# Delta-rule attention without the first segment's reading of an empty memory, with the memory's start multiplied in bf16

## The reference, cut to what matters

```python
def step(carry, seg):
    mem, z = carry
    qq, kk, vv = seg
    sigma_q = elu(qq) + 1.0
    att_dot = softmax(causal(qq @ kk.T / scale)) @ vv
    att_mem = sigma_q @ mem / (sigma_q @ z)
    sigma_k = elu(kk) + 1.0
    delta = vv - sigma_k @ mem / (sigma_k @ z)
    mem_new = mem + sigma_k.T @ delta
    z_new = z + sigma_k.sum(axis=-2)
    att = beta * att_mem + (1.0 - beta) * att_dot
    return (mem_new, z_new), att @ Wo
mem0 = zeros((H, DK, DV)); z0 = ones((H, DK, 1)) / DK
```

## Time and profile before

| what | us |
| --- | --- |
| median of 3 runs | 709.62 |
| lowest and highest of them | 709.52, 710.14 |
| the profiled execution | 709.2 |
| its span, first to last instruction | 706.7 |

### The profile page before, as it was taken

The page is one execution under the profiler, slowest core; times in us unless marked ns, Lnnn a source line. Parts: engine busy times, 40 slices in busy tenths (PEclk is TensorE's granted clock), DMA queues, the critical chain, the costliest instruction groups (busy, mean ns, idle before and its releaser), DMA issues. The chain is left out here.

```text
span 706.7 us, 12441 instructions
## 1 busy us (share of the span) xinstructions
PE 641.2 (91%) x4222; PEld 559.5 (79%) x4222; DVE 405.3 (57%) x1063; ACT 339.7 (48%) x836; POOL 309.8 (44%) x377
## 2 busy tenths in 40 slices
PE   4888999999999999999999998697999967997897
PEld 3677888988988988988988998575777756986675
DVE  6767387196296196295295463784223259635444
ACT  3665777567468567467567563221444321201221
POOL 4665562552552453453451020614777524301474
PEclk9999999999999999999999999899999979997799
DMA  8010010110210110200200132595333253008641
GB/s 265 34 62 31 31 42 21 55 32 13 62 36 1 64 33 0 65 31 0 68 1 1 38 83 68 180 410 165 103 103 105 83 182 120 1 0 302 219 121 44
DMA packets 29777, 57.89 MB, mean 82 GB/s; under 512 B 4670, under 2 KB 15904, under 8 KB 29728
## 3 DMA queue, kind: packets, MB, share of 16 engines
q1 hardware_dynamic: 22720, 42.03, 17.3%
q0 software_dynamic: 4896, 13.12, 6.4%
q10 hardware_dynamic: 2112, 2.10, 0.9%
HBM read 48.06 MB, written 10.09 MB: 82 GB/s over the span
## 5 line engine op out<-in xcount | busy, mean ns | idle before, releaser
L911 DVE RECIPROCAL denominators<-readings 128x2 f32<-128x2 f32 x128 | 21.1, 165 | 147.6 <-PE readings L587 146.6
L447 POOL TENSOR_TENSOR w_high<-xn,ones 128x256 fp32r<-128x256 f32 x84 | 53.9, 672 | 76.0 <-PE ahead L235 38.2
L587 PEld LDWEIGHTS readings<-memory_copy,sigma 128*128 128x128 f32 x512 | 75.4, 191 | 11.4 <-ACT memory_copy L784 2.2
L793 ACT ACTIVATE memory_reading<-readings,denominators 64x128 f32<-64x128 f32 x256 | 78.5, 356 | 6.0 <-DVE denominators L911 4.0
L587 PE MATMUL readings<-memory_copy,sigma 128*128 128x129 f32 x512 | 78.8, 276 | 2.2 <-ACT memory_copy L784 2.1
L784 ACT ACTIVATE memory_copy<-memory 128x258 f32<-128x258 f32 x128 | 50.3, 393 | 62.1 <-PE memory L597 48.1
L917 DVE SCALAR_TENSOR_TENSOR minus_delta<-readings,denominators,v 64x128 f32<-64x128 f32 x240 | 73.8, 347 | 4.5 <-DVE denominators L911 0.3
L597 PE MATMUL memory<-minus_delta,sigma_k_tokens 128*128 128x129 f32 x480 | 73.2, 275 | 0.0
L1221 POOL DMA_INDIRECT xs_e<-rows_e,gather_at_e x46 | 44.6, 969 | 55.3 <-DVE gather_at_e L1635 18.3
L451 POOL TENSOR_TENSOR w_low<-xn,w_high 128x256 fp32r<-128x256 f32 x84 | 65.7, 813 | 1.6
L769 ACT ACTIVATE x<-ahead 128x512 f32<-128x512 f32 x60 | 35.8, 597 | 62.1 <-PE ahead L235 28.8
(11 more groups left out here) (282 smaller groups left out, 1433.9 us busy)
## 6 DMA issues: line engine op xcount, KB each, us to landing
weights_e<-experts SPq DMA_DIRECT2D x24, 608.0 KB, 11.8
xn<-L_attn_Wq SPq DMA_DIRECT2D x8, 512.0 KB, 3.9
xn<-L_attn_Wk SPq DMA_DIRECT2D x7, 512.0 KB, 3.8
xn<-L_attn_Wv SPq DMA_DIRECT2D x7, 512.0 KB, 3.8
wo<-L_attn_Wo SPq DMA_DIRECT2D x1, 2048.0 KB, 13.2
rows_e<-xn ACTq DMA_DIRECT2D x4, 512.0 KB, 8.0
x<-L_attn_x SPq DMA_DIRECT2D x4, 256.0 KB, 3.2
x<-L_attn_x SPq DMA_DIRECT2D x2, 512.0 KB, 3.4
```

The lines of the kernel that those rows point to most:

```text
L447: last = pool.tensor_tensor(w_high[i][:, :, of], w_stage[:, :, of], one, ALU.mult)
L587: last = pe.matmul(KQ[g][:, hh * MC:(hh + 1) * MC], sqk[:, GROUP * g + hh, pair, 2 * par:2 * par + 2, :], mz[g][:, hh, :], start=True, sto ...
L793: last = act.activation(read[rows, half, GROUP * g + hh, pair, :], KQ[g][rows, hh * MC:hh * MC + DK], ACT.Copy, scale=nr[g][rows, hh:hh + 1])
```

## The change

`start` and a second identity (`ident16`) are bf16, and `seed` multiplies these. In a turn's first segment neither group reads its memory: the two `read_memory` calls, the copies of the memory for them, the scalings of the reading and the inversion are left out, and VectorE makes minus delta as -1 times v, in one instruction for the two heads of a group, waiting only for v. The rows of `read` that belong to the first segment are set to zero once, by POOL in `set_constants`. All counts of the semaphores go from 16 (or 8 a half) to 15 a turn.

```diff
-        start = sb("memory_start", [P, GROUP * MC])
+        start, ident16 = sb("memory_start", [P, GROUP * MC], BF16), sb("ident16", [P, P], BF16)
...
+        UPDATES = NSEG - 1
...
+                pool.tensor_copy(ident16[:, :], ident[:, :]).then_inc(consts_set, 1)
                 norm.set_power(pool)
...
-                    pool.wait_ge(consts_set, 11)
+                    pool.wait_ge(consts_set, 12)
+                    pool.memset(read[SEG:P, 0, :, 0, :], 0.0).then_inc(consts_set, 1)
+                    pool.wait_ge(consts_set, 13)
                     pool.memset(probs[:, :, :], 0.0).then_inc(consts_set, 1)
...
                 def seed(g):
 
-                    pe.matmul(MM[g][:, 0:GROUP * MC], ident[:, :], start[:, :], start=True, stop=True,
+                    pe.matmul(MM[g][:, 0:GROUP * MC], ident16[:, :], start[:, :], start=True, stop=True,
                               skip_group_check=True).then_inc(upd_ready[g], 1)
...
                         for at in range(STEPS):
                             s = half * STEPS + at
-                            read_memory(it, 0, s)
                             if s:
+                                read_memory(it, 0, s)
                                 update_memory(it, 1, s - 1)
                             else:
                                 seed(1)
                             slot(it, half, 2 * at, first, last)
-                            read_memory(it, 1, s)
+                            if s:
+                                read_memory(it, 1, s)
                             if s < NSEG - 1:
                                 update_memory(it, 0, s)
...
-                            copy_memory(it, 1, s)
-                            scale_reading(it, 0, s)
+                            if s:
+                                copy_memory(it, 1, s)
+                                scale_reading(it, 0, s)
                             slot(it, half, 2 * at, first, last)
                             copy_ahead(it, half, 2 * at + 1, last)
                             if s < NSEG - 1:
                                 copy_memory(it, 0, s + 1)
-                            elif not last:
-                                copy_memory(it, 0, NSEG)
-                            scale_reading(it, 1, s)
+                            if s:
+                                scale_reading(it, 1, s)
...
                 def step(it, g, s):
                     pair, par = s // 2, s % 2
                     rows = slice(par * SEG, (par + 1) * SEG)
-                    dve.wait_ge(kq_ready[g], 16 * it + s + 1)
+                    if s == 0:
+                        heads = v[rows, pair, GROUP * g * DK:GROUP * (g + 1) * DK].rearrange("p (h c) -> p h c", h=GROUP)
+                        dve.tensor_scalar(dl[g][par][rows, :, 0:DK], heads, -1.0, None, ALU.mult).then_inc(dl_ready[g], 1)
+                        return
+                    dve.wait_ge(kq_ready[g], UPDATES * it + s)
```

More of the change, by code:

```diff
@@ L458, in set_constants @@
                             rows = slice(par * SEG, (par + 1) * SEG)
-                            pool.wait_ge(consts_set, 3 + 2 * (2 * g + par))
+                            pool.wait_ge(consts_set, 4 + 2 * (2 * g + par))
                             pool.memset(dl[g][par][:, :, :], 0.0).then_inc(consts_set, 1)
-                            pool.wait_ge(consts_set, 4 + 2 * (2 * g + par))
+                            pool.wait_ge(consts_set, 5 + 2 * (2 * g + par))
                             pool.memset(dl[g][par][rows, :, DK:MC], -1.0).then_inc(consts_set, 1)
-                    pool.wait_ge(consts_set, 11)
+                    pool.wait_ge(consts_set, 12)
+                    pool.memset(read[SEG:P, 0, :, 0, :], 0.0).then_inc(consts_set, 1)
+                    pool.wait_ge(consts_set, 13)
                     pool.memset(probs[:, :, :], 0.0).then_inc(consts_set, 1)
@@ L584, in read_memory @@
                     pair, par = s // 2, s % 2
-                    pe.wait_ge(mem_copied[g], 16 * it + s + 1)
+                    pe.wait_ge(mem_copied[g], UPDATES * it + s)
                     for hh in range(GROUP):
@@ L594, in update_memory @@
                     pair, par = s // 2, s % 2
-                    pe.wait_ge(dl_ready[g], 15 * it + s + 1)
+                    pe.wait_ge(dl_ready[g], UPDATES * it + s + 1)
                     for hh in range(GROUP):
@@ L657, in slot @@
                             for g in range(2):
-                                pe.wait_ge(read_ready[g], STEPS * n)
+                                pe.wait_ge(read_ready[g], UPDATES * it + half * (STEPS - 1))
                         elif h == 1:
@@ L729, in _ @@
                 wait_copied("project", 11)
-                pe.wait_ge(consts_set, 12)
+                pe.wait_ge(consts_set, 14)
                 seed(0)
@@ L738, in _ @@
                         for g in range(2):
-                            pe.wait_ge(read_ready[g], STEPS * n)
+                            pe.wait_ge(read_ready[g], UPDATES * NQ)
                     elif h >= 2:
@@ L790, in scale_reading @@
                     rows = slice(SEG, P) if par == 0 else slice(0, SEG)
-                    act.wait_ge(nr_ready[g], 16 * it + s + 1)
+                    act.wait_ge(nr_ready[g], UPDATES * it + s)
                     for hh in range(GROUP):
@@ L857, in _ @@
                     (copy_sigma_k if what == "turn" else copy_projection)(0, 0, u, norm_banks[i % 4])
-                copy_memory(0, 0, 0)
                 all_turns(act, turn)
@@ L913, in step @@
                         return
-                    dve.wait_ge(nr_ready[g], 16 * it + s + 1)
+                    dve.wait_ge(nr_ready[g], UPDATES * it + s)
                     for hh in range(GROUP):
@@ L983, in _ @@
                 dve.wait_ge(beta_step, 3)
-                dve.wait_ge(consts_set, 12)
+                dve.wait_ge(consts_set, 14)
                 dve.wait_ge(mask_loaded, 16)
```

## The result

| what | us |
| --- | --- |
| changed kernel, median of 11 runs | 702.59 (700.46 to 704.52) |
| kernel before, 11 runs beside it | 708.52 (704.78 to 710.87) |
| ratio, 95% interval | 0.9922 (0.9904 to 0.9939) |
| the profiled execution after | 700.46, span 698.7 |

The profiled execution is the fastest of the 11, so that its trace leans to the favourable side.

The account below looks back on a forecast made before the run. TensorE's queue was taken to bound the attention. -4.62 for three later turns and +0.3 for POOL gave -4.3 us: 704.9 from the profiled execution, 705.3 from the median, so 705.2 was forecast, range 703.4 to 707.3.

Parts of the forecast that it names:

- Three later turns, 3 x 1.54 = 4.62: Starts of the three later turns: 0.88 + 0.66 = 1.54 us less of TensorE's queue each, 4.62 us in all.
- the seeds, 0.66 a turn start: Each bf16 seed at a turn's start was to cost 0.11 us instead of 0.44, saving 0.33 a seed.
- The readings' 0.88: One memory reading per group removed in each turn: 2 x 0.44 = 0.88 us of TensorE's queue.
- VectorE, ScalarE and the copies at nothing: At the turn starts, work removed from VectorE and ScalarE was costed at nothing, as both wait for TensorE there.
- the gain is absorbed: Rival, 0.06: VectorE's dense run doesn't move, so TensorE waits 0.60 + 1.54 us there in each later turn; 709.9 us.
- A seed that still costs 0.44: Rival, 0.04: bf16 seeds no cheaper, leaving 2.64 us less 0.3; 707.3 us.
- The 0.3 for POOL: First turn: VectorE's two multiplications hold up POOL's split by 0 to 0.56 us; 0.3 taken, delaying TensorE's gates.
- The first turn at nothing: First turn: no gain, since TensorE's gates at 39.32, 49.45 and 63.02 us wait for POOL's splits and their loads.
- The first rival: Rival, 0.13: the clock falls behind the first turn's longer wait before 39.3 us, costing up to 1.6; 706.9 us.
- the second: Rival, 0.12: TensorE, late by that fall, waits shorter before 63.02 and the fall at 64 stays out; 703.7 us.
- The base of the sum: The kernel before at 709.62 us, the median of the runs, from which the gain of 4.3 us was taken.
- Behind the attention: Sign of being wrong: a stage behind the attention changes its length by over 1 us.

Follow-up runs that it names:

- seeds only: The kernel before with the bf16 start and bf16 identity and nothing else of the change; 707.38 us, ratio 0.9969.
- one wait filled: The changed kernel with eleven filler products (results overwritten) in TensorE's first-turn wait for POOL's split; 705.08 us, ratio 0.9949.
- both waits filled: The changed kernel with eleven filler products in the first turn's wait for POOL's split and eight in its wait for the masked scores; 703.42 us, ratio 0.9935.
- warm start: The changed kernel with both first-turn waits filled, and 22 filler products ahead of TensorE's first work; 703.19 us, ratio 0.995.
- first turn reads: The changed kernel, but still reading its memory in the first turn; 703.44 us, ratio 0.993.

## Why the prediction came out as it did

**Three later turns, 3 x 1.54 = 4.62: right in kind, 8% too much.** They gave 1.48 + 1.38 + 1.39 = 4.25 in the first pair of traces, and 4.25 and 4.26 in the two other traces of the changed kernel against the first of the kernel before. The counts are those named: 480 readings and 8 bf16 seeds. The term that was mis-sized is the seeds, 0.66 a turn start, which gave 0.54 to 0.56 in *seeds only*. The first goes from 0.44 to 0.12 (134.28 to 134.40), as its 256-column neighbour promised; but the projection behind it takes 2.76 us to the next seed where it took 2.66 to what followed it. The second seed leaves 0.21 to the scores, not 0.11, and it had cost 0.53 (137.66 to 138.19), not the 0.44 that the prediction took for both. So 0.32 + 0.32 - 0.10 = 0.54. The readings' 0.88 measured 0.85 to 0.88.

**VectorE, ScalarE and the copies at nothing: right.** The copy of the memory ends 0.72 us ahead of the reading (141.56 to 142.28), where 0.70 had been worked out; the gate in the seventh slot moved along, so "the gain is absorbed" falls. "A seed that still costs 0.44" falls by the 0.12.

**The 0.3 for POOL: too much.** POOL's first split took 2.42 and 2.77 in place of 2.32 and 2.77, and its gate came 4.81 us behind the first seed, not 4.72: 0.1, not 0.3. At full clock even that is gone at the next gate, 14.84 us behind the first seed in *one wait filled* and 14.85 in the kernel before. VectorE was held up rather: its two multiplications took 1.27 us, where the fastest of the trace's eight took 0.28.

```profile
35.23 2.42 POOL L449 TENSOR_TENSOR w_high<-xn,ones 128x256 fp32r<-128x256 f32 x4 [2.86 <-PE local L235]
```

```profile
35.92 1.27 DVE L915 TENSOR_SCALAR minus_delta<-v 64x256 f32<-64x256 f32 x2 [2.07 <-ACT v L778]
```

By the Trainium skill's rule (SBUF — State Buffer, Who interferes with whom) the one of the two engines that issues first holds the shared port pair for its whole instruction and the other is blocked; the prediction had drawn from it that POOL would lose the full 0.56. POOL had begun 0.69 us before VectorE here (35.23 and 35.92), and VectorE lost the more by far, which agrees with the rule's order and not with the 0.56.

**The first turn at nothing: wrong, and this is the step that failed.** "I cost the gain of the first turn at nothing" gave 0 where the traces have 0.5 to 1.3 us. Two rivals that the prediction kept apart came together: the granted clock does fall (0.57 over 40 to 44) behind the new wait, which is 2.83 us and not 3.2, as the second seed waits 0.29 for ScalarE first; and because TensorE is then late, the fall at 64 stays out. The fillers show it: with the first wait filled the fall is back at 64. The rule of the Trainium skill that an idle TensorE falls back to its lower level (TensorE: Matmul & The Clock Gate, What's actually happening) agrees with the first; the time of 706.9 that the prediction gave for it took in no gain at 64. The first rival was to cost up to 1.6 and cost 0.4 to 1.1; the second was to give 1.6 and gave 1.6. The prediction had the place and the mechanism of both, but the sum went without them.

**The base of the sum, and the range.** The other step that failed is the base of the sum, 709.62, the median of three runs, and with it the argument that "the three timed runs lie within 0.62 us of each other". In all the runs of the kernel before, 125 of them, the median is 707.93 and they reach from 702.77 to 712.4; 33 runs of the changed kernel have 703.80 (700.46 to 707.55). So the forecast started 1.7 us too high, and its difference, -4.3, stands beside -4.1 between these medians. That these two agree is partly luck: the traces' turns come to 4.25 + (0.46 to 1.28) = 4.7 to 5.5 us. What takes up the rest in the medians isn't shown; the later start of the attention, 1.6 to 2.1 us in eight of ten traces, would be enough. The single comparison of 11 runs, -5.9 from 708.52, was at the favourable end: the two repeats gave ratios of 0.9936 and 0.9953. The range took in the unknown costs of the change but nothing for the spread of a median, which is 2.4 us over three of the changed kernel: 702.59, 705.01 and 704.28. With 703.80, or with either of the other two, the forecast's range would have held.

**Behind the attention: chance, not the change.** The prediction was to be wrong if a stage there changed by over 1 us; one did, and it says nothing of the change. What lies behind the attention is 253.74 to 257.97 us long over the 14 traces, in either kernel, whenever the attention ends. Stretches of low clock do come and go there, against the prediction's argument: worked out from the tables of stages as the prediction does at 64, TensorE is at 1.2 GHz for 34 to 52 us of it, and the three shortest traces have 34 to 35. In 114 executions of the kernel before the mean granted clock goes from 0.960 to 0.977, and a straight line through them gives 3.6 us for 0.01 of it (r = -0.71). On such lines the two kernels are 4.9 us apart at the same clock of 0.968 (708.6 and 703.8).

None of the other versions is faster than the changed kernel by more than these runs can tell: both waits filled, 703.42 and, with the warm start, 703.19, *first turn reads* 703.44, against 703.80.

## What to carry to other kernels

Where one engine leads without gaps, the distance from one start to the next is the price of an instruction, and removing two kinds of it gave the sum of their prices, in each repetition alike; the price depends on what stands behind the instruction, 0.44 or 0.53 us for the same seed, so it is read at each place; where it waits for others, the same removal only lengthens the wait. A wait that grows can still move the time, by where the clock falls afterwards: ask whether what follows has slack to take up the slow stretch. And three timed runs that agree within 0.1% say little about the spread, so a range needs a term for it, and one trace's gain in a stretch that the change doesn't touch needs a second trace.

## What was not expected of the hardware

A few products in a wait hold the clock: nineteen that nobody needs took the first turn from 99.64 (eleven of them) to 98.04 us, though the medians don't show the gain. A bf16 product of 258 columns is one instruction that lets the next start after 0.10 to 0.21 us, where the fp32 one was two in 0.44 and 0.53. And one and the same program spreads over 6 to 8 us between executions made one after the other, half of that variance going with the mean granted clock (r = -0.71).
